# Unused bf16 products on TensorE in its idle time ahead of the first expert slots of an audio tower

## The reference, cut to what matters

```python
h = _L0_tok_ref(x, L0_tok_W1, L0_tok_b1, L0_tok_W2, L0_tok_b2)
h = h + _L0_attn_ref(_layernorm(h), w_q, w_k, w_v, w_o)          # 16 heads, sequences of 32
h = h + _L0_ffn_ref(_layernorm(h), w_gate, w_expert, b_expert)   # 8 experts, capacity 100, top 1
h = h + _L1_attn_ref(_layernorm(h), phazor_real, ...)            # decayed, turning state
h = h + _L1_ffn_ref(_layernorm(h), Wg, W1, W2, W3)

def _L1_ffn_ref(x, Wg, W1, W2, W3):
    logits = xf @ Wg
    top_w, top_i = jax.lax.top_k(logits, 2)
    combine = ...                                                # softmax of the two
    y = jnp.einsum('enh,ehc->enc', silu(xf @ W1[e]) * (xf @ W2[e]), W3)
    return jnp.einsum('enc,ne->nc', y, combine)
```

## Time and profile before

| | |
|---|---|
| median of three runs | 519.73 us (519.11, 519.73, 519.74) |
| the profiled execution | 519.39 us |
| its span, first to last instruction | 517.62 us |
| TensorE (PE) busy | 429.8 us, 83% of the span |
| VectorE (DVE) busy | 288.5 us, 56% |
| ScalarE (ACT) busy | 208.0 us, 40% |
| GpSimd (POOL) busy | 162.0 us, 31% |
| mean granted clock of TensorE | 0.918 of full speed |

### The profile page before, as it was taken

The page is one execution under the profiler, slowest core; times in us unless marked ns, Lnnn a source line. Parts: engine busy times, 40 slices in busy tenths (PEclk is TensorE's granted clock), DMA queues, the critical chain, the costliest instruction groups (busy, mean ns, idle before and its releaser), DMA issues.

```text
span 517.6 us, 9150 instructions
## 1 busy us (share of the span) xinstructions
PE 429.8 (83%) x3287; PEld 280.5 (54%) x3292; DVE 288.5 (56%) x838; ACT 208.0 (40%) x389; POOL 162.0 (31%) x140
## 2 busy tenths in 40 slices
PE   0598999898767566547789999999999999999991
PEld 0244556456455346446546766676666666566661
DVE  0598877686869899978886488428411111111110
ACT  0244653463577414236334553346133323333230
POOL 6051010010101214431143536433535431554322
PEclk9999999899868956865689999999999999999997
DMA  9999110046054100822011522152322325232311
GB/s 177 251 213 204 38 38 3 9 133 231 18 169 186 44 3 3 314 92 83 2 49 22 123 37 46 29 136 30 52 41 42 49 52 182 43 59 44 47 21 20
DMA packets 36102, 43.14 MB, mean 83 GB/s; under 512 B 5216, under 2 KB 30560, under 8 KB 35904
## 3 DMA queue, kind: packets, MB, share of 16 engines
q1 hardware_dynamic: 26384, 32.14, 22.2%
q0 software_dynamic: 7488, 10.23, 12.2%
q10 hardware_dynamic: 2192, 0.27, 0.5%
HBM read 30.96 MB, written 11.53 MB: 82 GB/s over the span
## 4 chain that ended last, share of the span: by engine, by line
PE 63%; DVE 19%; DMA 7%; issue 5%; ACT 4%; SPq 1%; POOLq 0%; POOL 0%; DVEq 0%; ACTq 0%
PE psum L2243 23%; PE psum L2262 12%; PE psum L1878 8%; PE psum L2253 3%; DMA KT<-in_L_attn_w_o_dram 3%; PE psum L1904 2%; PE psum L1892 2%; DMA out_dram<-mixture_rows_out 2%; PE psum L1922 2%; PE psum L2233 2%; PE psum L1956 1%; DVE st_att L1044 1%; PE psum L1948 1%; DVE M2s L919 1%; DVE qtok L1190 1%
## 5 line engine op out<-in xcount | busy, mean ns | idle before, releaser
L1779 DVE TENSOR_TENSOR QT<-QT,psum 128x512 f32<-128x512 f32 x39 | 26.8, 688 | 139.0 <-PE psum L2243 138.9
L1878 PE MATMUL psum<-M2s,M1s 128*128 128x512 f32 x128 | 60.7, 619 | 20.6 <-DMA M1s<-in_L_tok_W_dram 18.5
L2243 PE MATMUL psum<-M1s,KT 128*128 x156 | 75.3, 606 | 0.9 <-ACT KT L827 0.7
L2262 PE MATMUL psum<-M3s,KT 128*128 x312 | 74.1, 380 | 1.2 <-ACT KT L835 0.8
L2243 PE MATMUL psum<-M2s,KT 128*128 x156 | 73.7, 595 | 0.0
L2262 PEld LDWEIGHTS psum<-M3s,KT 128*128 128x128 f32 x312 | 58.6, 190 | 22.1 <-issue 16.0
L846 ACT ACTIVATE O<-psum,gate_slot 128x256 f32<-128x256 f32 x39 | 18.5, 474 | 106.5 <-PE psum L2262 106.5
L504 POOL DMA_INDIRECT KT<-mixture_rows_in,src_i x39 | 41.8, 1071 | 37.5 <-issue 19.4
L2243 PEld LDWEIGHTS psum<-M2s,KT 128*128 128x128 f32 x156 | 29.9, 192 | 38.1 <-issue 38.1
L1878 PEld LDWEIGHTS psum<-M2s,M1s 128*128 128x128 f32 x128 | 23.8, 196 | 45.4 <-issue 25.3
L531 POOL DMA_INDIRECT mixture_rows_out<-O,src_i x17 | 30.8, 1810 | 32.9 <-ACT O L846 13.2
(11 more groups left out here) (406 smaller groups left out, 734.0 us busy)
## 6 DMA issues: line engine op xcount, KB each, us to landing
M3s<-in_x_dram SPq DMA_DIRECT2D x4, 1024.0 KB, 10.5
M3s<-in_L_ffn_W_dram SPq DMA_DIRECT2D x1, 4096.0 KB, 14.6
M2s<-in_L_ffn_W_dram SPq DMA_DIRECT2D x1, 4096.0 KB, 16.0
M1s<-in_L_ffn_W_dram SPq DMA_DIRECT2D x1, 4096.0 KB, 13.8
M3s<-in_x_dram SPq DMA_DIRECT2D x4, 992.0 KB, 14.4
M1s<-vtok SPq DMA_DIRECT2D x64, 34.0 KB, 1.9
mixture_rows_out<-H SPq DMA_DIRECT2D x4, 512.0 KB, 4.9
M1s<-in_L_tok_W_dram SPq DMA_DIRECT2D x2, 512.0 KB, 14.2
```

The costliest lines, as they stand in the source:

```text
L1779: v.tensor_tensor(sil[:, u, :], sil[:, u, :], bank[3], ALU.mult).then_inc(v_gated, 1)
L1878: last = mm(bank[6 + c], W1s[:, r, P * c:P * (c + 1)], xr[:, i % 2, r].rearrange("p b l -> p (b l)"), start=(n == 0), stop=(n == STRIDE - 1))
L2243: last = mm(z, xrT[:, u, c, :], w[:, bass.ds(e, 1), c, :].rearrange("p a h -> p (a h)"), start=(c == 0), stop=(c == CH - 1))
L2262: last = mm(bank[6][:, 0:DM], actT[:, u, c, :], M3s[:, bass.ds(e, 1), c, :].rearrange("p a d -> p (a d)"), start=(c == 0), stop=(c == HC - 1))
```

## The change

It puts 48 products into TensorE's program, in six places between `att_mean(3)` and `expert_rows(3)`. Each multiplies the bf16 identity with the 512 columns of `bias3` and writes a whole bank of PSUM, which the next real product into that bank overwrites; nobody reads the result. Two waits that TensorE's program holds anyway are repeated ahead of such a group (`v_ssm_added`, which also stands behind `places0(2)`, and `v_att_added`, which `expert_rows` begins with). Nothing else is changed.

```diff
+            def keep_busy(n, z):
+
+                for _ in range(n):
+                    mm(z, ident_b[:], bias3[:].rearrange("p a d -> p (a d)"), start=True, stop=True)
+
             last = STEPS - 1
             pe.wait_ge(v_att_rows, STEPS)
             state_rows(0, bank[4:6])
             att_mean(last)
             pe.wait_ge(a_expert, TS * last)
+            keep_busy(10, bank[2])
+            pe.wait_ge(v_ssm_added, 1)
+            keep_busy(10, bank[2])
             places0(2, bank[6])
             pe.wait_ge(v_ssm_added, 1)
             state_rows(1, bank[4:6])
             pe.wait_ge(a_norm3T, 2)
             pe.wait_ge(a_norm2T, last)
             norm4_columns(0, bank[0:2])
+            keep_busy(4, bank[2])
             logits(0, bank[2])
+            keep_busy(12, bank[7])
             att_columns(last)
             norm4_columns(1, bank[0:2])
             pe.wait_ge(v_kept, 3)
             att_proj(last)
             logits(1, bank[2][:, E * TS:])
             pe.wait_ge(v_ssm_added, 2)
+            keep_busy(8, bank[4])
             norm3_columns(2, bank[4:6])
             places2(0, 0, EARLY, 1, bank[2])
             norm2_columns(last)
+            pe.wait_ge(v_att_added, STEPS)
+            keep_busy(4, bank[6])
             expert_rows(last, range(0, 2))
             slot_tables(0, EARLY, FULL_EARLY, bank[3])
             expert_rows(last, range(2, TS))
```

## The result

The changed kernel took 516.80 us, the median of four runs (515.90 to 517.55), against 519.66 us before (519.11 to 519.74, four runs): a ratio of 0.9946 with a 95% interval of 0.9926 to 0.9967, so 2.8 us gained (1.7 to 3.8). The forecast was 517.8 us. The sign and the range held, but 516.80 lies outside the 517.2 to 518.8 us that the likeliest case alone was to give. The same kernel measured again beside the kernel before (e12, twelve runs) came to a ratio of 0.9966, 1.8 us gained (0.8 to 2.7); the two intervals overlap.

The account below looks back on a forecast made before the run. Bound: TensorE's half-clock work on the chain, then VectorE to the first `slot_gate`. Gains of 1.1 us (first twenty) and 1.34 us (rest), partly given back at the eight, left 1.85 us off 519.73: 517.9, rounded to 517.8 us; range 516.2 to 519.4.

Parts of the forecast that it names:

- the likeliest case: Clock back during the eight products or `norm3_columns`: middle gain 1.85 us, 517.2 to 518.8 us; forecast's chance 45%.
- The bound: Half-clock TensorE work on the chain, then VectorE to the first `slot_gate`; what that gains, the end gains.
- The first twenty: Ten products after `att_mean`, ten after the state rows: clock back by about 220.6, everything up to `oq` 1.1 us earlier.
- The hole ahead of `att_columns`: Behind the twelve products 3.0 us of idleness are left; the clock falls again between 233 and 236.
- T: The end of `places2`, 247.10 us before; with the clock back by then the gain is 248.44 - T.
- rival 1: Clock back for `logits(1)`, `places2` done at 245.0: gain 3.4 us, 516.3 us; chance 27%.
- The eight: Ahead of `norm3_columns(2)`: free if the clock is back for `logits(1)`, otherwise `norm3_columns` takes 1.7 us more.
- The half-clock case that the prediction priced: The eight run 242.2 to 245.6 at half clock, `norm3_columns` ends at 247.3, giving back the first gain wholly or partly.
- The rest: From the end of `places2` to `token_of`: at full clock VectorE's 6.35 us bound it, gaining 1.34 us for unchanged T.
- Rival 3: The first slot, `slot_up(0)` at half clock, swallows gain: 3.4 us becomes 2.3; 517.4 to 518.9 us; chance 9%.
- Rivals 2 and 4: Half-clock products stand in the way, 521.0 or 522.1 us, chance 9%; no effect, 519.2 to 520.2 us, chance 10%.
- rival 4: No effect: the products don't move the clock, or the hole undoes everything; 519.2 to 520.2 us; chance 10%.

Follow-up runs that it names:

- e12: The changed kernel itself measured again beside the kernel before, twelve runs; ratio 0.9966 to the kernel before.
- e7: Changed kernel plus 14 more products ahead of slot 0, behind the waits after the last `expert_rows`; ratio 0.9961 to the kernel before.
- e10: Changed kernel with 21 products instead of 12 ahead of `att_columns`, plus 14 ahead of slot 0 and 11 behind `slot_rows(1)`; ratio 0.9953 to the kernel before.
- e6: Changed kernel with 21 products instead of 12 behind `logits(0)`, ahead of `att_columns`; ratio 0.9937 to the kernel before.
- e8: Changed kernel with 21 products instead of 12 ahead of `att_columns` and 14 more ahead of slot 0; ratio 0.9975 to the kernel before, median 518.87 us.
- e5: Changed kernel with each product replaced by four bf16 transposes of the identity, 128 columns each; ratio 0.9940 to the kernel before.
- e2: Changed kernel with only the first twenty products, the other four groups taken out; ratio 0.9974 to the kernel before.
- e4: Changed kernel with only the eight ahead of `norm3_columns(2)` and the four ahead of `expert_rows`; ratio 0.9966 to the kernel before.
- e11: Changed kernel without the eight products ahead of `norm3_columns(2)`; ratio 0.9962 to the kernel before.

## Why the prediction was right, and where it was off

*The bound.* Right. What the first `slot_gate` gained the end gained, within 0.3 us, in all profiles but e7 (1.6 us lost) and e10 (0.5 us lost). One reading beside it was too short: the DMA share of 0 that I named holds only up to 227.42, and from there to 230.83 it is 0.90 again.

*The first twenty.* The profit was sized at 1.1 us; mask to `oq` went from 11.89 to 11.09 us, 0.8. ScalarE's copy starts at 227.67, 4.16 us behind the mask (4.97 before); it starts 0.58 us behind the end of the rows that `norm4_columns(0)` transposes, and not 0.34 as I had it. How it comes was wrong too: I had the clock fall at 217 and be brought back at 220.6. In each profiled execution with the twenty it did not fall there at all; it was held up. The groups were never too long for their gaps: 2.3 us, then 1.17 us idle, then 2.3.

*The hole ahead of `att_columns`.* I expected 3.0 us of idleness, and from it a fall between 233 and 236; measured were 2.04 us and a fall at 236.08. That the hole makes the fall is not borne out. In four of the nine profiles with the four, `logits(0)` and the twelve (or 21) behind the twenty, the clock fell ahead of the hole, at 230.11 to 231.49, during the last of the eight-column products of `logits(0)` or within 1.1 us behind them. In e12, the changed kernel again:

```profile
230.27 4.12 PE L2197 MATMUL psum<-bias,ident_b 128*128 128x512 bf16 x12
235.06 0.62 PE L1985 MATMUL psum<-ident_b,oq 128*128 128x128 bf16 x8 [0.67 <-DVE oq L1268]
```

```profile
231.49:234.90 3.41, 2.90 (x8) 0.50 0.01 2
```

In three others it fell at 235.49 to 236.08, behind the hole, and in e6 and e8, where 21 products fill it, not at all there. The hole was over-sized mostly because I gave `logits(0)` 0.9 us where my own row had 1.69 us at full clock; it took 1.95.

*The step that was mis-sized* is the return of the clock. The likeliest case had it come back during the eight products or `norm3_columns`, T of 246.6 and 1.85 us; "back for `logits(1)`", rival 1, had 27%. In every profile with all six groups it was back by then or within 0.5 us of the start of `logits(1)`: at 239.49, at 234.90, at 233.52 in e5. `logits(1)` took 2.00 us instead of 3.42 (timelines), VectorE became the bound as in rival 1, and `top_one` came 1.77 us earlier after the mask (1.95 worked out). My reason against it was that the same pieces did not bring it back in the kernel before. In e2 they did: there too the clock was down when `att_columns` began, and it was back at 238.89. What makes the difference between e2 and before is not settled; the pieces are the same and start 0.8 us sooner after the mask. Alone, the twenty and the sixteen are worth 1.5 us each in their profiles; all six groups together give 3.3.

*The eight.* Not in the way: they ran at full clock and ended at 242.93, 1.4 us before the last of ScalarE's rows. The half-clock case that the prediction priced occurs in e4, and there the price is repaid by the full clock behind them.

*The rest.* 1.34 us from the end of `places2` to `token_of` was nearly right, 1.42 came: 7.65 us before (247.14 to 254.79), 6.23 after. But the full clock is not needed all the way for it: e11 has the same 6.23 us with `norm2_columns` at half.

*The sum and the rivals.* 3.4 us was the most that the stretch could give, worked out from VectorE's chain, and 3.30 to 3.38 is what seven of the eight profiles with all six groups show up to `token_of` (e10: 2.73). Rival 3 took its part in the first profile, 0.66 us of 1.1 priced, and nothing in the second. With it came one of the signs by which the prediction called its forecast wrong: the first `slot_gate` waited for `slot_up(0)`. Rivals 2 and 4 didn't occur; e1 shows that rival 4 would be right for products of 8 columns. So the number held by way of a case that was not the likeliest one: rival 1 gave 3.3 us up to `token_of`, rival 3 took back 0.66. The range covers it because its lower end had been set by rival 1; that the gain measured again, 1.8 us, is close to my 1.85 is luck, since its profile went rival 1's way too. As the executions of both kernels scatter, the rest of the difference can't be laid to one term.

## What to carry to other kernels

Unused products pay where TensorE's slow clock is on the chain, and only up to the point where the next engine is the bound; work that bound out first, as no more can be gained. 48 products of 512 columns gained, 48 of 8 columns gained nothing (e1). Put wide ones where the idleness is certain, and size them for half clock if the clock may be down (21 products for a hole of 4.7 us were 1.5 us too long in e10). Before making TensorE arrive earlier at a wait, look at what it will do there: the idle time moves to the next wait (2.7 us in e7, 2.8 in e8), and if that stands ahead of a stretch that TensorE bounds, a fall of the clock there costs more than was won, as in e7's profile, though not in e8's.

## What the runs showed that I had not expected

Executions of programs that are identical up to 216 us arrive at the mask between 222.3 and 225.2 us (e4 and e8). The clock falls and returns at different moments ahead of it, for instance at half from 145.5 to 159.2 us in the kernel before and from 143.3 to 157.0 in e11; that this is the reason is not shown. Timed runs of the kernel before scatter as well: 517.0 to 521.5 us in the 31 runs beside e1 to e4. The two fastest of them had a mean granted clock of 0.929 and 0.926, the two slowest 0.915, so a part of the scatter goes with the clock. Time outside the span adds to it in some variants: 2.3 to 3.1 us in nine of twelve runs of e8, 2.5 to 2.8 in four of six of e5 and 2.0 to 2.8 in four of twelve of e7, against 1.7 to 1.9 elsewhere; the cause is open. A change worth 0.5% needs the stretches of the profile to be understood; twelve timed runs gave intervals of 0.3 to 0.5% width.

The changed kernel's two profiles differ by 0.7 us in this stretch, with the same instructions, by where `slot_up(0)` meets the half clock: from 256.56 to 263.38 in one, from 258.79 to 262.21 in the other.
